# The last key block's probabilities are added by VectorE before TensorE sums them, in a fused FFN, attention and FFN kernel

## The reference

```
x = x + 0.5 * ffn(layernorm(x))
x = x + attention(layernorm(x))          # 16 heads of 64, keys and values from a 32-wide latent
x = x + 0.5 * ffn(layernorm(x))

attn = softmax(where(key <= query, q @ k / 8, -inf), axis=keys)
y    = attn @ v ;  out = y @ Wout
```

## Time and profile before

| | us |
|---|---|
| median of 3 runs | 913.27 |
| lowest and highest | 913.05, 915.11 |
| profiled execution, its span from first to last instruction | 915.6 |

### The profile page before, as it was taken

How to read it: one execution, slowest core, us unless ns; L and a number is a source line. 1 busy time by engine, 2 the same in 40 slices (tenths; PEclk the granted TensorE clock), 3 DMA queues, 4 the chain that set the end, 5 groups by cost and what they waited for, 6 DMA issues and landing times. The chain is left out here.

```text
span 915.6 us, 21654 instructions
## 1 busy us (share of the span) xinstructions
PE 858.2 (94%) x7750; PEld 572.1 (62%) x7750; DVE 644.4 (70%) x1818; ACT 549.3 (60%) x1113; POOL 731.9 (80%) x834
## 2 busy tenths in 40 slices
PE   5688999999999999999999999999999999999886
PEld 4455666666576666666566666666666666657455
DVE  3387577678767677768767777876867767776645
ACT  4444666757666565756756665766656575655551
POOL 4304789898989989898898989898988989789732
PEclk9878999999999999999999999999999999999999
DMA  4446251523535151533535152443525153340000
GB/s 101 113 111 140 54 118 36 124 73 85 124 82 126 42 129 39 120 88 82 126 71 130 33 126 57 98 110 82 125 58 119 37 117 74 83 102 14 14 24 12
DMA packets 77546, 77.89 MB, mean 85 GB/s; under 512 B 9392, under 2 KB 51136, under 8 KB 77440
## 3 DMA queue, kind: packets, MB, share of 16 engines
q1 hardware_dynamic: 76640, 75.45, 35.5%
q10 hardware_dynamic: 800, 1.07, 0.4%
HBM read 9.90 MB, written 8.39 MB: 20 GB/s over the span
## 5 line engine op out<-in xcount | busy, mean ns | idle before, releaser
L483 POOL TENSOR_TENSOR first_probs<-first_probs,later_probs 128x768 f32<-128x768 f32 x240 | 371.2, 1555 | 23.7 <-PE bank L755 23.7
L593 ACT ACTIVATE later_probs<-bank 128x384 f32<-128x384 f32 (+1 forms) x448 | 231.0, 538 | 153.5 <-PE bank L742 152.5
L742 PE MATMUL bank<-q_stack,keys 123*128 123x512 f32 (+1 forms) x704 | 308.4, 463 | 9.8 <-ACT first_probs L593 8.3
L1059 DVE TENSOR_REDUCE maxima<-bank 128x1 f32<-128x512 f32 (+1 forms) x384 | 254.9, 682 | 67.5 <-PE bank L811 67.3
L811 PE MATMUL bank<-keys,q_stack 122*128 122x512 f32 (+3 forms) x1024 | 256.3, 338 | 11.6 <-issue 2.8
L811 PEld LDWEIGHTS bank<-keys,q_stack 122*128 122x128 f32 x1024 | 181.8, 193 | 103.0 <-issue 41.4
L593 ACT ACTIVATE first_probs<-bank 128x512 f32<-128x512 f32 x256 | 139.9, 594 | 106.1 <-PE bank L742 102.2
L1059 DVE TENSOR_REDUCE block_max<-bank 128x4 f32<-128x512 f32 x256 | 173.6, 678 | 39.8 <-PE bank L811 39.1
L742 PEld LDWEIGHTS bank<-q_stack,keys 123*128 123x128 f32 x704 | 127.9, 191 | 72.0 <-ACT first_probs L593 33.7
L516 POOL TENSOR_SCALAR_AFFINE_SELECT later_probs<-later_probs 128x512 f32<-128x512 f32 x192 | 124.1, 647 | 55.5 <-ACT later_probs L593 55.5
L755 PE MATMUL bank<-later_probs,lat 128*32 128x384 f32 (+2 forms) x1536 | 110.1, 389 | 0.7 <-POOL later_probs L516 0.7
(11 more groups left out here) (127 smaller groups left out, 831.2 us busy)
## 6 DMA issues: line engine op xcount, KB each, us to landing
q_stack<-q_high SPq DMA_DIRECT2D x256, 128.0 KB, 2.4
q_stack<-q_low SPq DMA_DIRECT2D x128, 128.0 KB, 2.5
out_dram<-x SPq DMA_DIRECT2D x32, 256.0 KB, 2.6
x_in<-in_L_attn_x_bld_dram SPq DMA_DIRECT2D x16, 256.0 KB, 3.2
x_back<-out_dram SPq DMA_DIRECT2D x16, 256.0 KB, 3.0
keys<-keys_staged SPq DMA_DIRECT2D x15, 192.0 KB, 2.5
keys<-keys_staged SPq DMA_DIRECT2D x30, 96.0 KB, 2.4
lat<-lat_staged SPq DMA_DIRECT2D x16, 64.0 KB, 1.9
```

What stands on the lines that cost most here:

```text
L483: nc.gpsimd.tensor_tensor(total, total, later_probs[j - 1][:, heads], ALU.add).then_inc(added, 1)
L593: nc.scalar.activation(probs_of(s)[:, e:e + heads, 0:n], score_bank(t, u)[:, 0:heads * n].rearrange("p (e q) -> p e q", e=heads), ACT.Exp) ...
L742: nc.tensor.matmul(score_bank(t, u)[:, 0:heads * n], keys[par][:, PLAIN_BLOCK[j], :], q_stack[par][:, first:first + heads, j * P:L], start ...
L1059: nc.vector.tensor_reduce(out, seg, AX.X, ALU.max).then_inc(a_free, 1)
```

## The change

VectorE gets a new addition for each group, `close_total`, at the end of its step 4g+4 (for group 3 that is step 0 of the next round). It adds `later_probs[2]`, 128x512 elements, onto the last 128 queries of the four heads in `first_probs`, and signals `closed`. TensorE's part over `later_probs[2]` at step 4g+5 goes away; the one at step 4g+6 now waits for `added` and `closed` and is otherwise as it was. ScalarE's exponential of the next group's block j = 3 waits for `closed` where it waited for `den_done`.

```diff
-WEIGH_ONES = [[], [2], [6], []]
+WEIGH_ONES = [[], [], [6], []]
-LAST_ONES = [[], [2, 5], [], []]
+LAST_ONES = [[], [5], [], []]
-DEN_PARTS = [3, 0]
+CLOSE_AT = 4
...
                         if j in ADDED:
                             wait_batch(act, added, t, 0, PARTS * G * len(ADDED),
                                        PARTS * ((g - 1) * len(ADDED) + ADDED.index(j) + 1))
+                        elif j:
+                            wait_batch(act, closed, t, 0, G, g)
                         else:
-                            wait_batch(act, den_done, t, 0, 2 * G, 2 * g - 1 if j else 2 * g - 2)
+                            wait_batch(act, den_done, t, 0, G, g - 1)
...
-                    if j == 0:
-                        wait_batch(pe, added, t, off, PARTS * G * len(ADDED), PARTS * (g + 1) * len(ADDED))
-                    else:
-                        wait_batch(pe, p_ready, t, off, STEPS, s + 1)
-                    for i in range(j, TT):
+                    wait_batch(pe, added, t, off, PARTS * G * len(ADDED), PARTS * (g + 1) * len(ADDED))
+                    wait_batch(pe, closed, t, off, G, g + 1)
+                    for i in range(TT):
...
+                def close_total(off, g):
+
+                    wait_batch(dve, pv_done, t, off, STEPS, g * TT + 1)
+                    wait_batch(dve, p_ready, t, off, STEPS, (g + 1) * TT)
+                    wait_batch(dve, added, t, off, PARTS * G * len(ADDED), PARTS * (g + 1) * len(ADDED))
+                    total = first_probs[g % 2][:, :, L - P:L]
+                    nc.vector.tensor_tensor(total, total, later_probs[-1][:], ALU.add).then_inc(closed, 1)
...
                     last_adds(s)
+                    if (s - CLOSE_AT) % TT == 0:
+                        if s >= CLOSE_AT and attend:
+                            close_total(0, (s - CLOSE_AT) // TT)
+                        if s < CLOSE_AT and end:
+                            close_total(-1, (s - CLOSE_AT + STEPS) // TT)
```

More of the change, by code:

```diff
@@ L262, in macaron_block @@
         added = sem("added")
+        closed = sem("closed")
         den_done = sem("den_done")
@@ L759, in weigh_ones @@
                 def weigh_ones(off, s):
-                    g, j = divmod(s, TT)
-                    if g == 0 and j == DEN_PARTS[0]:
+                    g = s // TT
+                    if g == 0:
                         wait_batch(pe, den_free, t, off, 1, 0)
@@ L765, in weigh_ones @@
                             pe.wait_ge(ones_made, G * TT)
-                    if j == 0 and t == B:
+                    if t == B:
                         stay_busy_by_columns(BUSY[0])
-                    if j == 0:
-                        wait_batch(pe, added, t, off, PARTS * G * len(ADDED), PARTS * (g + 1) * len(ADDED))
-                    else:
-                        wait_batch(pe, p_ready, t, off, STEPS, s + 1)
-                    for i in range(j, TT):
+                    wait_batch(pe, added, t, off, PARTS * G * len(ADDED), PARTS * (g + 1) * len(ADDED))
+                    wait_batch(pe, closed, t, off, G, g + 1)
+                    for i in range(TT):
                         for e in range(HG):
                             last = nc.tensor.matmul(den_bank[e * LD:(e + 1) * LD, 0:P], group_ones[:, g * TT + i, :],
-                                                    probs_of(s)[:, e, (i - j) * P:(i - j + 1) * P],
-                                                    start=(g == 0 and j == DEN_PARTS[0] and i == j),
-                                                    stop=(g == G - 1 and j == DEN_PARTS[-1] and i == TT - 1))
+                                                    first_probs[g % 2][:, e, i * P:(i + 1) * P],
+                                                    start=(g == 0 and i == 0), stop=(g == G - 1 and i == TT - 1))
                     last.then_inc(den_done, 1)
@@ L1086, in invert @@
                 def invert():
-                    wait_batch(dve, den_done, t, -1, 2 * G, 2 * G)
+                    wait_batch(dve, den_done, t, -1, G, G)
                     nc.vector.reciprocal(den_inv[:], den_bank[:, 0:P]).then_inc(den_free, 1)
```

## The result

The changed kernel took 958.74 us (median of four runs, 957.84 to 960.27). The kernel before, run beside it on the same chip, took 914.19 (913.05 to 915.45). The ratio is 1.0482, with a 95% interval of 1.0455 to 1.0509: slower by 4.8%, 44.6 us. The spans of the two profiled executions are 958.2 and 915.6, so the traces have 42.6 us to account for. The forecast was 942, with 955 as its upper end.

The account below looks back on a forecast made before the run. Each 52.0 us round was a relay: GpSimd's chain bounds 15.2 us, TensorE's stream 36.8. Terms 11.6 + 6.2 + 13.5 - 4.4 + 2 = +28.9 us on 915.6 give 944.5, less 2.3: 942, range 935 to 954.

Parts of the forecast that it names:

- What is saved: TensorE loses one block of 8 records a group: one spacing of equal blocks, 0.22 us, at most 14.1 us in all.
- What is added: One VectorE addition a group, 0.58 us if unheld; it ends 0.54 us behind GpSimd's select, lengthening the next multiplication 0.45.
- The rival in which the close gets its turn first: The close goes ahead of GpSimd's select; group 0 costs 0.40 us, group 2 0.63, total 930 us; chance 0.12.
- Group 0: Close waits for GpSimd's addition and select, delaying VectorE's shuffles and GpSimd's multiplications: `project_out` 0.83 us later in 14 rounds, 11.6.
- Group 1: Close does not wait but takes 0.58 us of VectorE; `front_unit(5)` comes 0.48 us later in 13 rounds, 6.2 in all.
- the bound by a longer GpSimd instruction: Upper bound: group 1's close can meet one of GpSimd's own instructions and cost 0.5 us more in 13 rounds.
- Group 3: Wait hidden by 2.17 us of VectorE idle time; `xb` 0.45 us longer, taken as hidden; 0.22 us saving kept.
- Group 2: Close waits for GpSimd, so `x3` ends at 587.43; `front_unit(7)` comes 1.04 us later in 13 rounds, 13.5 in all.
- The rivals that the wait does not reach TensorE: GpSimd's additions end before VectorE arrives, so only savings of 13.2 us are left: 900 us; chance 0.12.
- reaches it at group 1 alone: Only group 1 stalls, with `front_unit(5)` still late: -4.1 us, so 909 us; chance 0.06.
- kept savings: 15 x 0.22 us at the round's boundary and 5 x 0.22 in rounds 0 and 14, assumed without such stalls: -4.4.
- In the last batch: VectorE's own additions are on the path; four closes more, less savings, cost 1.8 to 4 us, taken as 2.

Follow-up runs that it names:

- experiments 1: Kernel before without TensorE's block over the fourth key block and with no addition in its place (denominators incomplete): 908.74 us against 914.41, ratio 0.9922.
- 12: Kernel before with only group 3's last block added by VectorE, all other groups and the last batch as before: 911.73 us against 916.33, ratio 0.9951.
- Experiment 4: Kernel before with close_total's three waits and behind them an addition of constant tiles into a spare tile, TensorE's blocks kept: 957.85 us against 916.33, ratio 1.0452.
- experiment 2: Kernel before with only close_total's three waits in its place, no addition: 922.38 us, ratio 1.0076.
- 3: Kernel before with one 128x512 VectorE addition of constant tiles into a spare tile in close_total's place, without waits, TensorE's blocks kept: 937.89 us, ratio 1.0251.
- experiment 5: Changed kernel with group 2's close_total moved behind x3's addition in VectorE's stream: 946.11 us, ratio 1.0337 to the kernel before.
- experiment 7: Changed kernel with the last batch as before, without close_total and with TensorE's two blocks: 952.92 us, ratio 1.0412 to the kernel before.
- experiment 6: Changed kernel with group 2's close_total moved behind x3 in round 14 alone: 959.28 us against 914.99 for the kernel before, ratio 1.0486.

## Why the prediction was wrong in size and right in sign

*What is saved: right.* One spacing, 0.22 us, in experiments 1 and 12 alike, not the 0.40 us of busy time and not the 0.33 us to the next score. The Trainium skill (TensorE: Matmul & The Clock Gate, section Back-to-back issue gap) gives about 81 ns for each matmul of 128 columns in a stream of weight load and matmul pairs. The trace does not agree: 0.22 us for 8 records is 28 ns each. The saving is swallowed wherever a stall follows, and kept at the boundary (-0.20 in the changed kernel).

*What is added: right.* The turns (select, close, next multiplication) and their lengths, 0.54 us and +0.43 us, are those that the earlier trace rows gave. The rival in which the close gets its turn first falls: in the steady rounds the select behind GpSimd's addition keeps its 0.63 us, the close ends 0.54 behind that select at groups 0, 2 and 3, and the multiplication is what becomes longer. By the Trainium skill (SBUF — State Buffer, section Who interferes with whom) the two block each other fully; the row agrees in that the addition ends only after the select, though it ends 0.54 us behind it and takes 0.66 when nothing is in the way, so part of it goes on before.

*Group 0: right.* +0.84 at `project_out`, forecast 0.83. *Group 1: right.* +0.53, forecast 0.48; the bound by a longer GpSimd instruction did not come. *Group 3: right.* `xb` takes 1.71 instead of 1.27 us and it is hidden:

```profile
566.44 1.00 DVE L1086 TENSOR_TENSOR first_probs<-first_probs,later_probs 128x512 f32<-128x512 f32 x1 [1.81 <-POOL first_probs L484]
566.87 1.71 POOL L534 TENSOR_TENSOR xb<-x_in,half_bias 128x512 f32<-128x512 f32 x1
568.67 0.69 DVE L1142 TENSOR_TENSOR x<-bank,xb 128x512 f32<-128x512 f32 x1 [0.63 <-issue]
```

*Group 2: the mechanism right, the term too small.* +1.23, forecast 1.04. I let TensorE go on 0.05 us behind the end of `x3`; it went on 0.14 behind (608.88 to 609.02). The other 0.1 us is GpSimd's two additions: from before to after they start 21.44 us later (604.63 against 583.19), `front_unit(5)` 21.34 later (595.68 against 574.34). 13 x 0.19 = 2.5 us.

*The rivals that the wait does not reach TensorE*, or reaches it at group 1 alone, fall with the three waits above. Experiment 4 shows that it is wait and addition together that reach it.

**The step that failed** is in the sum: "kept savings: ... 5 x 0.22 in rounds 0 and 14, which have no stall of this kind", and "In the last batch ... I take 2". Both treat rounds at the ends as steady rounds with less in them. Measured:

- Round 0: +1.3 in place of -0.7. Group 1's close waits there (VectorE idles 1.88 us ahead of it at 105.65), and `front_unit(5)` is 1.6 us later than TensorE's instructions ahead of it. At this place the wait alone costs 0.8 us (experiment 2), the addition alone 0.1 (3), both 1.6 (4). No batch is ahead of this one, so VectorE has no tail work that would bring it to the close later; that this is why it arrives early is argued from the code.
- Round 14: +4.3 in place of -0.4. TensorE waits for maxima behind close and `x3`, and then runs at the lower clock. Experiment 4 has +4.2 with no saving, experiment 5 takes half of it away by moving the close: 0.6 us of wait and 1.6 of clock, as shown below.
- The last batch: +6.2 in place of 2, shown by experiment 7, which gives 5.8 us back. I priced a VectorE addition; the price is TensorE's wait for it (7.2 us at three groups, where the kernel before waits 3.0 for its last additions), and the stretches at the lower clock behind it.

How much of this is the clock can be read from executions that have the same wait. In round 14 of experiments 5 and 6 TensorE waits 1.49 us for maxima and then has the same instructions to do. The first three rows are of experiment 5, the last three of experiment 6:

```profile
868.60:872.00 3.40, 3.39 (x48) 2.33 (x49) 2.30 (x4) 0.31 (x1) 1.77 (x1) 1.00 0.00 0
868.61 0.50 PE L811 MATMUL bank<-keys,q_stack 122*128 122x384 f32 x2 [1.49 <-DVE maxima L1059]
870.91 0.51 PE L811 MATMUL bank<-keys,q_stack 122*128 122x256 f32 x2
877.50:880.90 3.40, 3.40 (x39) 1.75 (x40) 1.43 (x3) 0.00 (x0) 1.16 (x1) 0.50 0.00 0
877.19 0.57 PE L811 MATMUL bank<-keys,q_stack 122*128 122x384 f32 x2 [1.49 <-DVE maxima L1059]
881.11 0.51 PE L811 MATMUL bank<-keys,q_stack 122*128 122x256 f32 x2
```

Between the starts of the two instructions lie 2.30 us at the full clock (experiment 5) and 3.92 at the lower one (experiment 6): one such stretch costs 1.6 us. The last batch gives the same price. Behind a wait of 2.07 us TensorE needs 5.11 us for the instructions up to its next FFN matmuls in the kernel before (880.50 to 885.61, with a stretch at the lower clock), and 3.49 us for the same in the last experiment (876.51 to 880.00, with none). And from `project_out` of round 15 to that of round 16 the changed kernel takes 35.0 us with 13.7 us at the lower clock. Experiment 5 has the same waits for the closes there (1.62 and 1.65 us) and takes 32.4 with 3.4 us at the lower clock. So about 1.6 us of round 14 and 2.6 of the last batch are the clock's, 4.2 of the 10.3 us behind `project_out` of round 14; most of the rest is waits. What decides whether a wait is followed by the lower clock stays open.

## What to carry to other kernels

On an engine that works strictly in order, a wait and an instruction can cost more together than the sum of both, since each was partly hidden by the same slack (0.8% and 2.5% alone, 4.5% together): price what stands behind them, by the time from its end to the first engine that waits for it. Add up the first and the last rounds by their own instruction streams, not as steady rounds: here the last tenth of the span held two thirds of the miss. And a saving is kept only at the places where the shortened engine is the one waited for, so a change that pays at one of four places is best made at that one.

## What the runs showed of the hardware that was not expected

TensorE's clock fell to its lower level behind a wait of 2.12 us (878.73), while in the 13.4 us ahead of it, this wait among them, TensorE had been busy for 11.39 us at the full clock. The wait alone does not decide it: behind 1.49 us the clock fell in experiment 6 and not in experiment 5, and behind 2.07 us in the kernel before and not in the last experiment. Neither the kernel before nor the changed one, whose waits there are 1.2 us at most, falls in its steady rounds. One stretch of 3.4 us at the lower level cost 1.6 us.

A small GpSimd instruction pays for VectorE's turn as a large one does: `t_var`, on 128x4 elements, took 0.67 us beside the close of group 1 (593.56), where `t_shift`, of the same shape and kind, took 0.23 us right behind it (594.31).
